# Graph network, edge convolutions: the gathers' waits moved from TensorE's counters to VectorE's

## The chip, the cores and the metric

The kernel runs on one core of a Trainium2 chip. The metric is device microseconds of one execution; the median of three runs is 2301.54 us (2296.12 to 2301.65). Four names are used for engines: TensorE (PE in the profile; PEld is its weight load), VectorE (DVE), ScalarE (ACT) and GpSimd (POOL). SP is the engine that only issues DMAs here.

## The reference, cut to what matters

There are 3125 nodes with 96 features and 53125 directed edges, sorted by destination. Four graph layers follow each other, each with a residual sum and a layer norm: two hops of normalised neighbour sums, two edge convolutions, sixteen hops with a teleport term, and two graph convolutions with a graph norm between them. The change is in the edge convolutions only:

```python
msg = x[src] @ W_msg + edge_attr @ W_edge             # one message per edge
agg = jax.ops.segment_max(msg, dst, num_segments=x.shape[0])
agg = jnp.where(jnp.isneginf(agg), 0.0, agg)
return agg + x @ W_root + b                           # leaky_relu behind it, twice in a row
```

## The kernel before, in words

A convolution is the function `edge_conv`, called twice. `x @ W_msg` is computed first for all nodes (`node_product`), kept in the on-chip memory (`y`, the tile `rows`) and also written to DRAM (`messages`), as two half-precision parts of 96 columns side by side. The edges are then walked in 26 turns (`N_IT`) of 16 tiles of 128 edges. The row `x[src] @ W_msg` of every edge of a tile is fetched in one of two ways:

- Eleven tiles of a turn (`FROM_POOL`) are gathered by GpSimd: one indirect DMA per tile (L1423) takes 128 rows from `messages` in DRAM into `conv_rows`. The tiles of a turn are j = 0 to 10; there are two sets of buffers, so the gathers of turn i + 2 go into the buffers of turn i.
- The five others (`TAKEN`) are taken by TensorE. VectorE writes one-hot matrices (L1540, 25 instructions a turn, in eight chunks: seven of three and one of four), TensorE multiplies them with `y` (L1473, 125 matmuls a turn, in the same eight chunks) and ScalarE evacuates the result (L1595). The one-hots lie in a ring of four slots (three of three tiles, one of four): VectorE may fill chunk h only when TensorE has finished chunk h - 4.

A message group is four tiles. TensorE starts it with the edge attributes (L1452) and adds the fetched rows with the identity (L1461, L1462). VectorE runs a segmented running maximum over it (L1550, the scan), TensorE turns the result back (L1500), and ScalarE evacuates it and stores it to DRAM (L1603, L1605). SP loads attributes and masks three groups ahead (L1374, L1376).

The order is written out by hand on each engine. For turn i, TensorE runs: message group 0, takes 0 and 1 of turn i + 1, message group 1, takes 2 and 3, the turn back of group 0, message group 2, takes 4 and 5, the turn back of group 1, message group 3, takes 6 and 7, the turn back of group 2. VectorE runs: scan 0, one-hots 4 and 5 of turn i + 1, scan 1, one-hots 6 and 7 of turn i + 1, scan 2, one-hots 0 and 1 of turn i + 2, scan 3, one-hots 2 and 3 of turn i + 2.

GpSimd runs only the gathers here, in order. From the third turn on (i >= 2), the first gather into each message group's buffers (j = 0, 4, 8) waits until the group two turns earlier has been computed. On top of that, every gather waits in `room(i - 2, j)`, which spreads the eleven gathers over a turn. It uses four counters. `s_msg` counts message groups, starting at 4. `s_scan` counts scans, starting at 4. `s_took` counts chunks of takes, seven a turn (the last chunk of a turn counts on another counter). `s_hot` counts chunks of one-hots, `NC` = 8 a turn. Before the change, with `step, late = divmod(j, 3)`, the gather waits for message group `step` of turn i - 2 if `late` is 0, and otherwise for chunk of takes 2 `step` + `late` - 1 of turn i - 1, which TensorE runs right behind that message group.

The gathers of the first two turns wait for none of this (turn 0) or for the first takes (turn 1). Behind the last gather, GpSimd fetches the first rows of the result, each waiting for late message groups and stores.

Of the kernel before, what the change touches and what calls it, by code (L numbers as in the profile page):

```python
# [60 lines left out]
GT = 4  # L61
# [6 lines left out]
NC = len(CHUNKS)  # L68
# [1247 lines left out]
def edge_conv(c, tag, y, result, head, sem, ends=False):  # L1316
# [14 lines left out]
    with ExitStack() as st:  # L1331
# [5 lines left out]
        def taken_rows(j, n):  # L1337
# [15 lines left out]
        s_zero, s_msg, s_scan, s_tr, s_back, s_hot, s_took, s_pair, s_evac = (  # L1353
            sem(f"{tag}_{n}") for n in ("zero", "msg", "scan", "tr", "back", "hot", "took", "pair", "evac"))
# [11 lines left out]
        with nc.Block(no_gpsimd_drain=True) as block:  # L1366
            @block.sync
            def _(sp):
                def load_group(i, g, width):
                    n = i * GT + g  # L1370
                    k = n % AHEAD
                    sp.wait_ge(s_msg, n + 1 + GT - AHEAD)
                    for q in (0, AE // 2):
                        sp.dma_start(attr[q:q + AE // 2, k, 0:width], halves_v[:, n * GW:n * GW + width]).then_inc(s_ea[k], 16)  # L1374
                    sp.wait_ge(s_scan, n + 1 + GT - AHEAD)
                    sp.dma_start(mk[:, k, 0:width], c["mask_d"][:, n * GW:n * GW + width].to_broadcast([F, width])).then_inc(s_mk[k], 16)  # L1376

                head.load_srcs(sp, 1, TE)
                if ends:
                    sp.wait_ge(s_none, 1)  # L1380
                    sp.dma_start(c["scan_d"][EP:EP + 1, :], none).then_inc(s_none, 16)
                for i in range(N_IT):
                    if i == 2:
                        if ends:
                            sp.wait_ge(s_ends, 1)
                        sp.dma_start(need[:, :], c["deg"][P - 1:P, :].bitcast(I32)).then_inc(s_need, 16)
                    for g in range(GT):
                        load_group(i, g, LEFT if i == last_it and g == GT - 1 else GW)
                        if g == 1 and i + 2 < N_IT:
                            head.load_srcs(sp, i + 2, LEFT_TAKEN if i + 2 == last_it else TE)  # L1390
                sp.wait_ge(s_pair, NB * N_IT)
                result.early(sp)

            @block.gpsimd
            def _(pool):
                for s in (s_msg, s_scan, s_tr, s_back):
                    pool.sem_inc(s, GT)
                for s in s_st:
                    pool.sem_inc(s, 16)
                pool.wait_ge(head.s_y, N_STORED)  # L1400

                def room(i, j):

                    step, late = divmod(j, 3)
                    if late == 0:
                        pool.wait_ge(s_msg, (i + 1) * GT + step + 1)
                    else:
                        pool.wait_ge(s_took, (i + 1) * (NC - 1) + 2 * step + late)

                def behind_first_takes(j):  # L1410

                    pool.wait_ge(s_took, 1 + j * (NC - 2) // (FROM_POOL - 1))

                for i in range(N_IT):
                    for g, tiles in enumerate(by_dma):
                        for j in tiles:
                            if i == 1:
                                behind_first_takes(j)
                            if i >= 2:
                                if j % GT == 0:  # L1420
                                    pool.wait_ge(s_msg, (i - 1) * GT + g + 1)
                                room(i - 2, j)
                            pool.indirect_dma_start(  # L1423
                                out=gat[:, i % 2, j, :], out_offset=None, in_=c["y_d"],
                                in_offset=bass.IndirectOffsetOnAxis(ap=idx_all[:, i * IT + j:i * IT + j + 1], axis=0),
                            ).then_inc(s_gat[i % 2][g], 16)

                pool.wait_ge(s_need, 16)
                if ends:
                    pool.wait_ge(s_none, 17)  # L1430
                pool.sem_inc(s_gate, 1)
                for k in range(2):
                    for g, tiles in enumerate(by_dma):
                        early = [k * FROM_POOL + j for j in tiles if k * FROM_POOL + j < EARLY]
                        if early:
                            stored = pool.value_load(need[0:1, early[-1]:early[-1] + 1], min_val=32, max_val=16 * (N_IT * GT // 2 + 1))
                            pool.wait_ge(s_msg, (N_IT - 2 + k) * GT + g + 1 + GT)
                            pool.sem_inc(s_gate, 1)
                            for parity in range(2):
                                pool.wait_ge(s_st[parity], stored)  # L1440
                                pool.sem_inc(s_gate, 1)
                            for t in early:
                                result.gather(pool, t)
# [481 lines left out]
```

## Time and profile before

| | |
|---|---|
| median of three runs | 2301.54 us |
| the profiled execution | 2304.43 us, span 2302.6 us |
| mean granted TensorE clock | 0.960 |
| TensorE, VectorE, ScalarE, GpSimd busy | 2030.8, 1240.7, 672.1, 759.0 us |
| the takes, L1473 | 639.2 us of matmuls, x6500 |
| the gathers of messages, L1423 | 578.3 us, x572 |
| the one-hots, L1540 | 346.3 us, x1300 |
| the scans, L1550 | 264.5 us, x208 |

The span runs from the first to the last instruction. The first convolution lies between about 286 and 760 us of it, the second between about 831 and 1306 us. Busy time of TensorE counts pipelined matmuls, so it says that the engine had work and not that it ran at its peak. "issue" as a releaser stands for idle time in which an engine waited for nothing that the profile shows, and "remote" for an event that the profile can't put to an instruction.

### The profile page before, as it was taken

The page shows a single profiled execution, that of the slowest core. Times are in us where ns is not written, and L with a number is a line of the kernel's source. Part 1 is how long each engine was busy: PE and PEld are TensorE (multiplying, and loading weights), DVE is VectorE, ACT ScalarE, POOL GpSimd, SP SyncE. Part 2 cuts the span into 40 slices and gives each one's busy share as a digit, 9 for nine tenths or more (in the row PEclk, how much of TensorE's full clock was granted, in tenths as well). Part 3 has the DMA queues.
Part 4 walks back from the last instruction along what each step waited for, and adds up shares of the span by engine and source line. Part 5 has one row for each costly group of instructions (what it writes and reads, how often), then busy time and mean ns, then how long its engine had stood idle before and what let it go on. Part 6 is the DMA issues. An engine that isn't in the chain of part 4 may idle for free. (4 is left out here: it accounts for less than half of the span.)

```text
span 2302.6 us, 57334 instructions
## 1 busy us (share of the span) xinstructions
PE 2030.8 (88%) x23524; PEld 1924.2 (84%) x23524; DVE 1240.7 (54%) x3485; ACT 672.1 (29%) x1939; POOL 759.0 (33%) x762
## 2 busy tenths in 40 slices
PE   4599688888888678888888699999999999999998
PEld 4499578777777567777777599999999999999988
DVE  8946366566565446666656474444444444444635
ACT  6824122222221212222222133332333333333434
POOL 2567366666555266656566510000000000000000
PEclk9999899999999789999999899999999999999999
DMA  3054445545554435555455400000000000000000
GB/s 75 1 164 131 106 123 137 132 132 132 131 133 117 122 87 134 134 131 133 130 132 130 126 17 2 2 2 2 2 2 2 2 2 2 1 2 2 2 2 23
DMA packets 153147, 163.58 MB, mean 71 GB/s; under 512 B 43697, under 2 KB 141612, under 8 KB 152885
## 3 DMA queue, kind: packets, MB, share of 16 engines
q1 hardware_dynamic: 100493, 83.89, 14.3%
q0 software_dynamic: 20464, 32.18, 7.5%
q10 hardware_dynamic: 31928, 43.84, 5.3%
q8 instruction: 186, 3.05, 0.5%
q14 instruction: 76, 0.62, 0.1%
HBM read 100.90 MB, written 58.89 MB: 69 GB/s over the span
## 5 line engine op out<-in xcount | busy, mean ns | idle before, releaser
L1473 PE MATMUL c_taken<-rows,conv_hot 125*128 125x192 f16 x6500 | 639.2, 253 | 102.7 <-issue 92.3
L1423 POOL DMA_INDIRECT conv_rows<-messages,idx_all x572 | 578.3, 1011 | 411.7 <-issue 121.6
L1473 PEld LDWEIGHTS c_taken<-rows,conv_hot 125*128 125x128 f16 x6500 | 555.7, 101 | 153.2 <-issue 137.3
L1540 DVE TENSOR_SCALAR conv_hot<-head_offset_srcs 125x640 f16<-125x640 f16 x1300 | 346.3, 328 | 272.2 <-DMA c_mask<-segment_mask 90.5
L1726 PE MATMUL l_ps<-rows,counts 125*128 125x192 f16 x5625 | 466.2, 246 | 1.9 <-DVE rows L1830 1.9
L1726 PEld LDWEIGHTS l_ps<-rows,counts 125*128 125x128 f16 x5625 | 464.0, 98 | 2.4 <-DVE rows L1830 2.4
L1726 PE MATMUL l_ps<-conv_rows,counts 125*128 125x192 f16 x5000 | 414.0, 246 | 0.8 <-DVE conv_rows L1871 0.8
L1726 PEld LDWEIGHTS l_ps<-conv_rows,counts 125*128 125x128 f16 x5000 | 412.6, 98 | 1.0 <-DVE conv_rows L1871 1.0
L1550 DVE TENSOR_TENSOR_SCAN c_scanned<-c_mask,c_scanned,c_msg 96x512 f32<-96x512 bf16 x208 | 264.5, 1272 | 151.0 <-DMA c_need<-deg 55.3
L1862 DVE SCALAR_TENSOR_TENSOR l_uf<-l_ps,l_cf,l_wide 125x96 f32<-125x96 f32 x400 | 127.1, 318 | 317.6 <-ACT l_wide L1797 317.6
L1603 ACT ACTIVATE c_back<-c_tr 128x384 f32<-128x384 f32 x208 | 102.0, 491 | 536.0 <-PE c_tr L1500 180.6
L1797 ACT ACTIVATE l_wide<-l_ps,l_cl 125x96 f32<-125x96 f32 x400 | 135.6, 339 | 294.3 <-PE l_ps L1726 286.5
L1500 PE MATMUL c_tr<-ident,c_scanned 96*128 96x96 f32 x832 | 112.1, 253 | 42.0 <-issue 34.9
L1462 PE MATMUL c_msg<-ident,conv_rows 128*96 128x128 f16 x728 | 118.0, 226 | 11.0 <-issue 10.7
L1461 PE MATMUL c_msg<-ident,conv_rows 128*96 128x128 f16 x728 | 117.4, 225 | 10.2 <-issue 10.0
L1500 PEld LDWEIGHTS c_tr<-ident,c_scanned 96*128 96x128 f32 x832 | 84.5, 144 | 49.0 <-issue 47.6
L1462 PEld LDWEIGHTS c_msg<-ident,conv_rows 128*96 128x96 f16 x728 | 88.3, 128 | 35.6 <-issue 17.6
L1868 DVE TENSOR_TENSOR l_uf<-l_uf,l_wide 125x96 f32<-125x96 f32 x400 | 103.0, 258 | 13.6
L1461 PEld LDWEIGHTS c_msg<-ident,conv_rows 128*96 128x96 f16 x728 | 90.6, 129 | 12.0 <-issue 11.9
L1595 ACT ACTIVATE conv_rows<-c_taken 128x384 f16<-128x384 f32 x104 | 42.8, 411 | 182.8 <-PE c_taken L1473 138.7
L1801 ACT ACTIVATE conv_rows<-l_uf 125x96 f16<-125x96 f32 x200 | 56.6, 283 | 135.5 <-DVE l_uf L1868 135.5
L1871 DVE SCALAR_TENSOR_TENSOR conv_rows<-conv_rows,l_uf 125x96 f16<-125x96 f16 x200 | 51.8, 259 | 69.9 <-ACT conv_rows L1801 69.9
(297 smaller groups left out, 1774.3 us busy)
## 6 DMA issues: line engine op xcount, KB each, us to landing
running_max<-c_back ACTq DMA_DIRECT2D x208, 192.0 KB
c_attr<-attr_halves SPq DMA_DIRECT2D x412, 64.0 KB
c_mask<-segment_mask SPq DMA_DIRECT2D x206, 96.0 KB
conv_rows<-messages,idx_all POOLq DMA_INDIRECT x572
head_srcs<-sources SPq DMA_DIRECT2D x50, 160.0 KB
l0a_raw<-in_ea_t SPq DMA_DIRECT2D x50, 132.8 KB, 2.3
attr_halves<-l0a_hi SPq DMA_DIRECT2D x50, 66.4 KB, 2.1
attr_halves<-l0a_lo SPq DMA_DIRECT2D x50, 66.4 KB, 2.1
```

What stands on the lines that cost most here:

```text
L1423: pool.indirect_dma_start(out=gat[:, i % 2, j, :], out_offset=None, in_=c["y_d"], in_offset=bass.IndirectOffsetOnAxis(ap=idx_all[:, i * IT ...
L1461: pe.matmul(to, row[:, 0:F], ident16[:, :], start=False, stop=False)
L1462: last = pe.matmul(to, row[:, F:2 * F], ident16[:, :], start=False, stop=(j == GT - 1))
L1473: return pe.matmul(acc[:, (NB * i + j // 2) % ACCS, j % 2 * (2 * F):(j % 2 + 1) * (2 * F)], hot[:, slot + k, j * ET:(j + 1) * ET], y[:, t, :],
L1500: last = pe.transpose(tr[0:ET, g % 2, j * F:(j + 1) * F], scanned[0:F, g % 2, j * ET:(j + 1) * ET], ident[0:F, 0:F])
L1540: last = v.tensor_scalar(hot[:, SLOTS[h % len(SLOTS)] + k, :], off[:, :], float(t * P - SRC_MID), None, ALU.is_equal)
L1550: v.tensor_tensor_scan(scanned[0:F, k, :], mk[:, n % AHEAD, :], msg[0:F, k, :], scanned[0:F, 1 - k, GW - 1:GW], ALU.add, ALU.max).then_inc ...
L1603: act.activation(back[:, g % 2, :], tr[0:ET, g % 2, 0:GT * F], ACT.Copy, scale=1.0 / YS).then_inc(s_back, 1)
L1726: return pe.matmul(ps[:, bank, at_col:at_col + 2 * F], at[:, k, t * P:t * P + 128], u[hop % 2][:, k, :], start=(k == 0 and at_col == 0), s ...
L1797: act.activation(clo[:, b, :], result(hop, t, 1), ACT.Copy, scale=(cl if hop < count else cl_next)[:, t:t + 1]).then_inc(s_clo, 1)
L1862: v.scalar_tensor_tensor(uf[:, t, :], result(hop, t, 0), (cf if hop < count else cf_next)[:, t:t + 1], clo[:, b, :], ALU.mult, ALU.add).th ...
L1868: v.tensor_tensor(uf[:, t, :], uf[:, t, :], xa[:, t, :], ALU.add).then_inc(s_uf, 1)
```

## The change

It replaces the two counters in `room`, which is called as `room(i - 2, j)` for every gather of turn i from the third turn on. If `late` is 0 the gather waits for scan `step` of turn i - 2, in place of message group `step`. Otherwise it waits for a chunk of one-hots: counted from chunk 0 of turn i - 1 it is chunk 3 + 2 `step` + `late`. For j = 1, 2, 4, 5 these are chunks 4, 5, 6, 7 of turn i - 1, and for j = 7, 8, 10 chunks 0, 1, 2 of turn i. The waits on `s_msg` for the buffers (j = 0, 4, 8) stay.

```diff
                     step, late = divmod(j, 3)
                     if late == 0:
-                        pool.wait_ge(s_msg, (i + 1) * GT + step + 1)
+                        pool.wait_ge(s_scan, (i + 1) * GT + step + 1)
                     else:
-                        pool.wait_ge(s_took, (i + 1) * (NC - 1) + 2 * step + late)
+                        pool.wait_ge(s_hot, (i + 1) * NC + 4 + 2 * step + late)
```

## Rows read from the trace of the kernel before

**Rows 1.** The page, part 1: busy us, share of span, instructions.
```profile
PE 2030.8 (88%) x23524; PEld 1924.2 (84%) x23524; DVE 1240.7 (54%) x3485; ACT 672.1 (29%) x1939; POOL 759.0 (33%) x762
```
**Rows 2.** Windows: stretch, length, busy us, PEclk, DMA share, GB/s.
```profile
323.80:727.90 404.10, 350.57 (x3897) 318.26 (x3896) 252.29 (x641) 86.95 (x177) 246.29 (x242) 0.96 0.52 132
870.00:1274.00 404.00, 348.18 (x3897) 314.48 (x3895) 251.46 (x638) 86.81 (x176) 243.56 (x242) 0.97 0.52 132
1310.00:2300.00 990.00, 969.83 (x11761) 963.92 (x11761) 447.68 (x1597) 324.20 (x1119) 13.05 (x12) 0.99 0.02 6
```
**Rows 3.** Groups by line, 323.8 to 727.9 us: busy, mean ns, idle before.
```profile
L1423 POOL DMA_INDIRECT conv_rows<-messages,idx_all x242 | 246.8, 1020 | 159.0 <-issue 53.3 <-remote 51.8 <-PE c_msg L1462 34.3
...
L1540 DVE TENSOR_SCALAR conv_hot<-head_offset_srcs 125x640 f16<-125x640 f16 x553 | 147.0, 327 | 100.4 <-remote 69.3 <-PE c_taken L1473 25.8 <-issue 3.3
L1550 DVE TENSOR_TENSOR_SCAN c_scanned<-c_mask,c_scanned,c_msg 96x512 f32<-96x512 bf16 x88 | 111.9, 1272 | 52.4 <-remote 40.5 <-PE c_msg L1462 9.2 <-issue 2.4
...
L1473 PE MATMUL c_taken<-rows,conv_hot 125*128 125x192 f16 x2750 | 266.5, 252 | 34.8 <-issue 29.3 <-ACT c_evacuated L1595 4.0 <-ACT conv_rows L1595 0.4
L1462 PE MATMUL c_msg<-ident,conv_rows 128*96 128x128 f16 x308 | 49.8, 226 | 4.2 <-issue 4.0
L1461 PE MATMUL c_msg<-ident,conv_rows 128*96 128x128 f16 x308 | 49.8, 225 | 2.8 <-issue 2.7
L1500 PE MATMUL c_tr<-ident,c_scanned 96*128 96x96 f32 x354 | 46.7, 249 | 10.0 <-issue 10.0
L1452 PE MATMUL c_msg<-c_attr,head_we 128*96 128x512 f16 x89 | 35.0, 393 | 1.8 <-issue 1.8
```
**Rows 4.** Lines L1540 and L1423: ns min/median/max, first and last start.
```profile
L1540 DVE TENSOR_SCALAR conv_hot<-head_offset_srcs x1300: 255/320/561, 253.9 to 1283.6; 125x640 f16<-125x640 f16 x186
...
L1423 POOL DMA_INDIRECT conv_rows<-messages,idx_all x572: 938/945/2523, 256.2 to 1274.6; - x191
```
**Rows 5.** Timeline of GpSimd: start us, us, instruction, idle before and releaser.
```profile
416.46 0.94 POOL L1423 DMA_INDIRECT conv_rows<-messages,idx_all  x1 [1.66 <-remote]
417.71 1.45 POOL L1423 DMA_INDIRECT conv_rows<-messages,idx_all  x1 [0.30 <-issue]
419.45 0.95 POOL L1423 DMA_INDIRECT conv_rows<-messages,idx_all  x1 [0.30 <-issue]
420.71 0.94 POOL L1423 DMA_INDIRECT conv_rows<-messages,idx_all  x1 [0.30 <-issue]
...
427.43 0.94 POOL L1423 DMA_INDIRECT conv_rows<-messages,idx_all  x1 [0.30 <-issue]
```
**Rows 6.** Timeline of VectorE, scans and one-hots of two stretches.
```profile
416.37 1.27 DVE L1550 TENSOR_TENSOR_SCAN c_scanned<-c_mask,c_scanned,c_msg 96x512 f32<-96x512 bf16 x1
417.56 1.48 DVE L1540 TENSOR_SCALAR conv_hot<-head_offset_srcs 125x640 f16<-125x640 f16 x6
420.37 1.27 DVE L1550 TENSOR_TENSOR_SCAN c_scanned<-c_mask,c_scanned,c_msg 96x512 f32<-96x512 bf16 x1 [1.34 <-remote]
...
439.70 1.27 DVE L1550 TENSOR_TENSOR_SCAN c_scanned<-c_mask,c_scanned,c_msg 96x512 f32<-96x512 bf16 x1 [2.41 <-remote]
440.90 1.71 DVE L1540 TENSOR_SCALAR conv_hot<-head_offset_srcs 125x640 f16<-125x640 f16 x7
...
446.31 1.77 DVE L1540 TENSOR_SCALAR conv_hot<-head_offset_srcs 125x640 f16<-125x640 f16 x6
```
**Rows 7.** Timeline of TensorE: a hole in the takes, a later message group.
```profile
428.39 0.49 PE L1473 MATMUL c_taken<-rows,conv_hot 125*128 125x192 f16 x4 [0.18 <-issue]
...
450.80 0.38 PE L1452 MATMUL c_msg<-c_attr,head_we 128*96 128x512 f16 x1
```
**Rows 8.** The page, DMA issues: KB each or us to landing.
```profile
counts<-edge_values,b_begin POOLq DMA_INDIRECT x5, 9.2
```
**Rows 9.** Timeline of all engines: a gather beside one-hots.
```profile
399.81 0.78 DVE L1540 TENSOR_SCALAR conv_hot<-head_offset_srcs 125x640 f16<-125x640 f16 x3
399.82 1.59 POOL L1423 DMA_INDIRECT conv_rows<-messages,idx_all  x1 [0.30 <-PE c_taken L1473]
```

## The prediction

> **What bounds the kernel now.** I read the page's busy times first [rows 1]: TensorE is busy for 88% of the span, VectorE for 54%, GpSimd for 33%. The change touches only the two convolutions, so the next view is the windows [rows 2]. They show 404.1 us and 404.0 us for the two stretches from the third to the twenty-fourth turn, each with 3897 matmuls. In each such stretch TensorE takes 2750 one-hot matmuls [rows 3], which is 22 turns of 125, so a turn lasts 404.1 / 22 = 18.37 us. Behind the convolutions, from 1310 us on, TensorE is busy 970 of 990 us, with 2% DMA [rows 2]; no gather of messages runs there, and nothing can change.
>
> The groups by line of the first stretch [rows 3] give each engine's load in one turn. GpSimd: 246.8 / 22 = 11.2 us of gathers. VectorE: (147.0 + 111.9) / 22 = 11.8 us, with (100.4 + 52.4) / 22 = 6.9 us idle. TensorE waits for no gather and for no one-hot: its idle time is put down to "issue" (29.3 + 4.0 + 2.7 + 10.0 + 1.8 = 47.8 us, or 2.2 us a turn) and to ScalarE's evacuation (4.4 us, 0.2 a turn). The timeline shows such an "issue" hole at 428.39 [rows 7]. So the conv is set by TensorE's own stream and by stalls that this trace cannot explain. GpSimd is a side queue, and the question is how much cover its gathers have.
>
> **What the change removes, adds and moves.** No instruction comes or goes: per conv, 24 turns x 11 = 264 gathers (528 of 572 in all) keep one wait each, against another counter. The four with j = 0, 3, 6, 9 wait for the scan behind the message group that they waited for; the seven others wait for the chunk of one-hots four chunks ahead of the chunk of takes that they waited for. By the code each new event lies behind the old one: the scan starts after its message group, and VectorE may fill a chunk's slots only after the very chunk of takes that the gather waited for (takes 0 and one-hots 4, takes 1 and one-hots 5, ..., takes 6 and one-hots 2 of the next turn). So every release comes later by the VectorE step, 1.27 us for a scan and 3 x 0.24 = 0.7 us or a little more for a chunk, and by whatever VectorE has queued ahead of it. It never comes earlier in itself.
>
> One turn, worked through. The gathers for the turn that starts at 447 start at 416.46, 417.71, 419.45 [rows 5]. The scan they would wait for ends at 416.37 + 1.27 = 417.64, the two chunks behind it at about 418.3 and 419.04 (417.56, six one-hots in 1.48), the next scan at 420.37 + 1.27 = 421.64 [rows 6]. A gather takes 0.94 us and the next starts 0.30 us behind its end [rows 4, 5]. The new starts are then 417.7, 418.95, 420.2 and 421.7: later by 1.2, 1.2, 0.75, and 1.0 against the fourth, which started when the queue was free. The middle ones gain less: those released by one-hots are already held by the queue ahead of them (427.43 would stay within 0.2 us [rows 5]). The last two and the next turn's first are again some 1.2 late. I take a mean of 0.6 us, with ends of 0 (all held by the queue) and 1.3 us (a full scan each).
>
> *What hides it.* The gather at 427.43 (j = 7) ends at 428.37 and feeds the second message group of its turn, which starts at 450.80 [rows 5, 7]: 22.4 us of cover. The message gathers' landing has no row; the longest median for another indirect gather is 9.2 us [rows 8]. 22.4 - 9.2 - 1.3 = 11.9 us are left. Cost on the path: 0. If the cover were gone, a shift would cost its own size once per turn at most, and only once per conv as a constant lag, for the lag doesn't add up as long as GpSimd keeps pace.
>
> *Does it keep pace?* It needs 11.2 + 11 x 0.30 = 14.5 us of 18.37 [rows 3, 5], so 3.9 us are free. Behind a waiting gather stand only gathers, and at the end those of the results, which wait for later message groups anyway. Nobody else waits for GpSimd there. Nothing is moved past SP's queue: its loads wait for the same counters as before.
>
> *What else moves.* The four scan-released gathers now start when VectorE turns to one-hots, and no longer beside the scan. Both kinds of meeting are in the trace already: a gather that started 0.01 us behind a one-hot took 1.59 instead of 0.94 us [rows 9], and one-hots run from 255 to 561 ns with a median of 320 [rows 4]. Bounds for one gather: 0 and +0.65 us on GpSimd; for its partner on VectorE: -0.06 and +0.24 us. The mean gather is 1.020 us long and the mean one-hot 0.327 [rows 3], so I take the small end on both: +0.1 us a gather, 1.1 us a turn out of GpSimd's 3.9, and under 0.1 us a turn for VectorE out of its 6.9 idle. Cost: 0. Gathers' packets move by half a microsecond in a conv whose DMA share is 0.52 [rows 2]; I bound that by plus or minus 0.1 us a turn and take 0.
>
> Here a rule bears on the change. The trace: a gather just behind the start of a one-hot was longer by 0.65 us, about a chunk of three [rows 9], but no one-hot was longer than 0.561 [rows 4]. The Trainium skill, "SBUF — State Buffer", section "Who interferes with whom", says that a VectorE operation in a two-port mode (tensor_scalar can be one) and a GpSimd operation shut each other out for the whole instruction, whichever came first. The first row agrees, the 0.561 does not: by the rule it should reach a gather's 0.94. By the rule's first half, all seven late gathers would be long ones: 11 x (0.945 + 0.30) + 7 x 0.65 = 18.3 us a turn, as good as the whole 18.37, so GpSimd would just keep pace and the cost would still be 0.
>
> **The sum.** 0 + 0 + 0 on the profiled execution's 2304.4 us (span 2302.6 and 1.8 around it). It stands 2.9 us above the median of 2301.5; the forecast is the median, 2302.
>
> **The rivals.**
> *S, slower: VectorE's one-hots stretch where VectorE sets the pace.* There are stretches in which VectorE has no wait: from 439.70 to 448.08 scans and one-hots follow each other directly [rows 6]. If each of the seven late gathers stretches one one-hot from 0.320 to 0.561, a turn gains 7 x 0.24 = 1.7 us of VectorE. The average turn swallows it; one in six may not: 8 x 1.7 = 14, so 2316. It decides from 0.14 us a turn over 48 turns. For it: the start of a gather is now tied to the start of the next one-hots. Against: TensorE shows no wait for one-hots at all [rows 3].
> *B, slower: the whole-instruction block.* If a gather that comes first shuts VectorE out for its 0.94 us, seven a turn add 6.6 us to 11.8: 18.4 us, the whole of today's turn, and any wait for TensorE comes on top. With 1 us of such waits, 48 x 1 = 48, so 2350. This is the second half of the rule above in the Trainium skill's "SBUF — State Buffer". Against it the 561 ns [rows 4].
> *F, faster: the "issue" stalls shrink.* If they have to do with when gathers fire, a twentieth to a fifth of 2.2 x 48 = 106 us might go; with a tenth, 2291. For it: they are the largest loss in the conv. Against: no row ties them to a gather, and two convs with different histories took 404.1 and 404.0 us.
> *N: the waits change nothing that can be seen.* Most gathers are held by the queue ahead of them and start where they did. Same time as my forecast, other reason: to be told apart by the starts.
>
> **How the numbers follow.** The forecast with N holds 0.64, F 0.15, S 0.17, B 0.04. A measurement of this kernel tells some 0.3% from no change, 6.9 us. Small drifts of the forecast beyond that are inside the shares: faster 0.17, same 0.62, slower 0.21. The range goes from F's 2290 to S's 2316 and leaves B and larger forms of F and S out, under 2 in 10.
>
> **What would show it right or wrong.** Right: gathers start about 0.6 us later against their scans, none before its scan's end; the idle time ahead of them is put down to VectorE; the message groups' idle stays without a gather; 22 turns in 404 us (401 to 407); the mean gather under 1.15 us, the mean one-hot at 0.32 to 0.34. Wrong: TensorE idle ahead of L1461 on a gather (the cover was not there), a mean one-hot above 0.36 with longer turns (S or B), or an "issue" idle in L1473 and L1500 that falls well under 40 us for the 22 turns (F).

## The result, and the profile after

The changed kernel takes 2368.38 us (median of four runs, 2362.52 to 2383.13) against 2301.6 us. The ratio is 1.0303, with an interval of 1.0278 to 1.0328: slower by 3.0%, and outside the range. The profiled execution took 2363.13 us, with a span of 2361.3 us; that is 58.7 us more than before. One of the ten runs of e17 below (2502.65 us, at a granted clock of 0.763) was slow and is left out of its ratio.

The first part of the page of the changed kernel answers to [rows 1]:

```profile
PE 2071.4 (88%) x23524; PEld 1956.1 (83%) x23524; DVE 1239.9 (53%) x3485; ACT 672.9 (28%) x1939; POOL 776.7 (33%) x762
```

VectorE and ScalarE work as long as before. TensorE is busy 40.6 us longer with the same number of matmuls, and the mean granted clock fell from 0.960 to 0.937.

```profile
core 0: 2361.3 us, clock 0.937
```

The windows of the third to the twenty-fourth turn of each convolution (columns as in [rows 2]):

```profile
324.00:756.70 432.70, 371.17 (x3896) 335.35 (x3895) 251.63 (x640) 87.04 (x177) 250.91 (x241) 0.90 0.49 123
902.10:1330.80 428.70, 364.19 (x3897) 328.25 (x3896) 251.17 (x639) 87.27 (x178) 255.21 (x242) 0.92 0.48 125
```

The same 22 turns take 432.7 and 428.7 us where they took 404.1 and 404.0 [rows 2]: 28.6 + 24.7 = 53.3 of the 58.7 us are here. A turn lasts 19.7 and 19.5 us instead of 18.37. The 53.3 us split in two: TensorE's busy time grew by 20.6 + 16.0 = 36.6 us for the same matmuls, and its idle time by the other 16.7 us. The clock is 0.90 and 0.92 instead of 0.96 and 0.97, so the first part is work at 1.2 in place of 2.4 GHz. The traces bear this out: at 2.4 GHz a matmul of these stretches adds 0.086 to 0.087 us of busy time in both kernels, and at 1.2 GHz 0.15 to 0.16; what grew is the number at 1.2, from 191 to 474 and from 136 to 368.

The groups by line of the first stretch (columns and order as in [rows 3]):

```profile
L1473 PE MATMUL c_taken<-rows,conv_hot 125*128 125x192 f16 x2750 | 282.7, 260 | 42.7 <-issue 41.5 <-ACT conv_rows L1595 0.5
L1423 POOL DMA_INDIRECT conv_rows<-messages,idx_all x241 | 252.4, 1047 | 182.1 <-issue 64.2 <-DVE c_scanned L1550 46.4 <-DVE conv_hot L1540 45.7
...
L1540 DVE TENSOR_SCALAR conv_hot<-head_offset_srcs 125x640 f16<-125x640 f16 x552 | 148.5, 329 | 135.0 <-remote 74.4 <-PE c_taken L1473 53.1 <-issue 7.0
L1550 DVE TENSOR_TENSOR_SCAN c_scanned<-c_mask,c_scanned,c_msg 96x512 f32<-96x512 bf16 x88 | 112.0, 1273 | 46.1 <-remote 36.1 <-PE c_msg L1462 6.0 <-issue 3.8
L1462 PE MATMUL c_msg<-ident,conv_rows 128*96 128x128 f16 x308 | 50.1, 227 | 4.7 <-issue 4.7
L1461 PE MATMUL c_msg<-ident,conv_rows 128*96 128x128 f16 x308 | 49.8, 227 | 1.9 <-issue 1.9
L1500 PE MATMUL c_tr<-ident,c_scanned 96*128 96x96 f32 x354 | 49.0, 258 | 7.7 <-issue 7.7
```

The mean gather is 1047 ns (1020 before) and the mean one-hot 329 (327). Of GpSimd's idle time 92 us are now put down to VectorE's two lines, as the diff says. No matmul waits for a gather. TensorE's idle time on "issue" grew, from 47.8 to 59.3 us (in its list of waits 41.5 for the takes, 7.7 for the turns back, 4.9, 3.3 and 1.9 for the message groups), and with it the mean take, from 252 to 260 ns.

What stands where such a hole lies? The timeline of GpSimd in the changed kernel shows seven gathers back to back, 0.30 us between two of them:

```profile
348.94 0.99 POOL L1423 DMA_INDIRECT conv_rows<-messages,idx_all  x1 [3.20 <-PE c_msg L1462]
350.23 1.34 POOL L1423 DMA_INDIRECT conv_rows<-messages,idx_all  x1 [0.30 <-issue]
351.88 0.96 POOL L1423 DMA_INDIRECT conv_rows<-messages,idx_all  x1 [0.31 <-issue]
...
356.90 0.95 POOL L1423 DMA_INDIRECT conv_rows<-messages,idx_all  x1 [0.30 <-issue]
```

TensorE's timeline beside it, from the last undisturbed takes on:

```profile
351.69 2.84 PE L1473 MATMUL c_taken<-rows,conv_hot 125*128 125x192 f16 x29
354.80 0.24 PE L1473 MATMUL c_taken<-rows,conv_hot 125*128 125x192 f16 x1 [0.27 <-issue]
...
356.29 0.29 PE L1500 MATMUL c_tr<-ident,c_scanned 96*128 96x96 f32 x1 [0.52 <-issue]
357.01 0.38 PE L1452 MATMUL c_msg<-c_attr,head_we 128*96 128x512 f16 x1 [0.43 <-issue]
...
359.15 0.34 PE L1461 MATMUL c_msg<-ident,c_evacuated 128*96 128x128 f16 x1 [0.36 <-issue]
...
359.60 3.73 PE L1473 MATMUL c_taken<-rows,conv_hot 125*128 125x192 f16 x22
```

And the windows before the holes, in them, and at the lower clock behind:

```profile
345.00:352.50 7.50, 6.46 (x81) 6.08 (x79) 5.12 (x14) 0.98 (x2) 3.69 (x4) 1.00 0.50 134
352.50:359.20 6.70, 4.15 (x33) 2.52 (x31) 1.75 (x3) 1.32 (x2) 4.13 (x5) 0.86 0.52 126
357.40:364.20 6.80, 5.92 (x37) 5.33 (x38) 3.66 (x10) 0.98 (x2) 3.37 (x5) 0.50 0.49 125
```

The train starts at 348.94 and its last gather ends at 357.85. From 354.5 to 359.15, so from 5.6 us behind its start to 1.3 us behind its end, TensorE gets one or a few instructions at a time, whatever they are: takes, turns back, message groups. 81 matmuls in 7.5 us become 33 in 6.7. Right behind it the granted clock is 0.50 (1.2 GHz) and 22 takes last 3.73 us, where 29 lasted 2.84.

I call gathers less than 0.35 us apart a train, and counted over both convolutions from the third turn on: 32 trains of five or more before, 54 after; pauses of over 0.25 us between the starts of two weight loads of TensorE (each less the 0.08 us of an undisturbed one), 195 us in all before and 219 after; time at 1.2 GHz, 136 us before and 249 after. The last four depend on where a convolution is taken to start and end, by up to 15 us; their differences, 24 and 113 us, hardly do. In the kernel before, a train of one gather had 0.12 us of such holes beside it on average, of three 0.80, of four 1.25, of five 2.07, of six 3.30. And at the start of its second convolution, where the wait under study doesn't apply yet, sixteen gathers run back to back from 803.0 to 822.7. The window of the kernel before:

```profile
805.00:838.00 33.00, 20.82 (x173) 16.23 (x172) 10.30 (x35) 1.92 (x4) 21.10 (x23) 0.72 0.27 60
```

173 matmuls in 33 us, at the rate of [rows 2] some 318, with all 12.2 us of idle time on "issue". So the trace of before held the mechanism; I had looked at one hole, and not at what GpSimd did ahead of it.

### The profile page after: what moved, and what is told of

Its sections match the earlier page's. It is cut to its first block and busy times, and to the rows that moved or that the text cites. A ratio compares the mean times of both kernels' runs of the same rounds, so it can differ in the third digit from the quotient of the medians.

```text
span 2361.3 us, 57334 instructions
## 1 busy us (share of the span) xinstructions
PE 2071.4 (88%) x23524; PEld 1956.1 (83%) x23524; DVE 1239.9 (53%) x3485; ACT 672.9 (28%) x1939; POOL 776.7 (33%) x762
## 5 line engine op out<-in xcount | busy, mean ns | idle before, releaser
L1473 PE MATMUL c_taken<-rows,conv_hot 125*128 125x192 f16 x6500 | 673.3, 260 | 132.6 <-issue 128.4
L1423 POOL DMA_INDIRECT conv_rows<-messages,idx_all x572 | 597.5, 1045 | 452.8 <-issue 155.4
L1473 PEld LDWEIGHTS c_taken<-rows,conv_hot 125*128 125x128 f16 x6500 | 578.3, 103 | 191.4 <-issue 178.5
L1540 DVE TENSOR_SCALAR conv_hot<-head_offset_srcs 125x640 f16<-125x640 f16 x1300 | 348.3, 329 | 339.7 <-PE c_taken L1473 132.9
L1461 PEld LDWEIGHTS c_msg<-ident,conv_rows 128*96 128x96 f16 x728 | 92.0, 131 | 14.3 <-issue 14.1
L1452 PE MATMUL c_msg<-c_attr,head_we 128*96 128x512 f16 x208 | 85.0, 409 | 7.3 <-issue 5.3
```

Source lines behind the costliest of these rows:

```text
L1423: pool.indirect_dma_start(out=gat[:, i % 2, j, :], out_offset=None, in_=c["y_d"], in_offset=bass.IndirectOffsetOnAxis(ap=idx_all[:, i * IT ...
L1461: pe.matmul(to, row[:, 0:F], ident16[:, :], start=False, stop=False)
L1473: return pe.matmul(acc[:, (NB * i + j // 2) % ACCS, j % 2 * (2 * F):(j % 2 + 1) * (2 * F)], hot[:, slot + k, j * ET:(j + 1) * ET], y[:, t, :],
L1540: last = v.tensor_scalar(hot[:, SLOTS[h % len(SLOTS)] + k, :], off[:, :], float(t * P - SRC_MID), None, ALU.is_equal)
```

## The experiments

The theory (T): gathers back to back starve TensorE's instruction stream, and the new releases make longer trains. Rivals: the gathers come too late (L); VectorE and GpSimd meet at the on-chip memory (P; the expectations below speak of its form with one-hots as V). Ratios are against the kernel before on the same chip.

**A train by itself, e1 (chip 12) and e5 (chip 4).** The gathers are added in the sixteen hops, where TensorE otherwise runs without a hole and there are no one-hots, scans or messages. `train(h, n)` puts n gathers into hop h; SP's twelve plain transfers are in hop 5:

```diff
...
+                train(2, 12)
+                train(3, 12, each_tile=True)
+                train(4, 12, kind="direct")
...
+                train(6, 12, kind="write")
+                train(7, 12, in_flight=1)
+                train(8, 12, in_flight=2)
+                train(9, 2)
+                train(10, 4)
+                train(11, 6)
```

> The kernel before, with gathers added to hops 2 to 11 of the sixteen-hop stage, where TensorE runs a matmul every 0.082 us with no hole and no other transfer is under way. The gathers fetch rows that nobody reads. Hop 2: 12 gathers back to back. Hop 3: 12 gathers, one per tile (2.06 us apart). Hop 4: 12 plain transfers of the same size from GpSimd. Hop 5: 12 plain ones from SP. Hop 6: 12 small memsets of GpSimd. Hop 7: 12 gathers, each waiting for the landing of the one ahead. Hop 8: at most two under way. Hops 9, 10, 11: 2, 4 and 6 back to back. Theory T (a long unbroken train of gathers starves TensorE): holes of 0.7 us in TensorE's stream in hop 2, some 6 to 9 us of them for 12 gathers, from 4 to 5 us behind the start to about 2.3 us behind the last start; about 0 for two, 1 for four, 3 for six; none or little in hops 3 and 7. Rival V (the gathers stretch one-hots and VectorE then holds TensorE): no one-hots here, so no hole in any hop. Rival L (lateness of the gathers): no hole, since nobody waits for them. Each hop lasts 51.7 us without holes.

The windows of e1, in this order: 12 gathers back to back; 12 gathers one per tile (2 us); 12 plain transfers from GpSimd; the same from SP; 12 gathers with at most two under way; then two, four and six gathers back to back.

```profile
1440.60:1457.80 17.20, 9.05 (x86) 6.92 (x84) 1.96 (x8) 1.53 (x5) 11.41 (x12) 0.80 0.17 35
1504.80:1529.00 24.20, 24.20 (x296) 24.20 (x294) 9.78 (x36) 7.21 (x24) 11.29 (x12) 1.00 0.13 27
1556.20:1567.00 10.80, 10.80 (x134) 10.80 (x132) 4.36 (x16) 3.12 (x10) 6.58 (x12) 1.00 0.23 57
1607.10:1615.00 7.90, 7.90 (x99) 7.90 (x97) 3.02 (x12) 2.50 (x8) 0.00 (x0) 1.00 0.36 77
1762.60:1783.00 20.40, 20.40 (x250) 20.40 (x248) 8.17 (x30) 6.24 (x20) 11.36 (x12) 1.00 0.14 31
1814.20:1819.00 4.80, 4.80 (x61) 4.80 (x59) 1.72 (x6) 1.45 (x5) 1.85 (x2) 1.00 0.09 21
1865.70:1872.00 6.30, 5.91 (x72) 5.69 (x71) 1.78 (x7) 1.59 (x5) 3.79 (x4) 1.00 0.17 35
1917.80:1927.00 9.20, 7.14 (x82) 6.40 (x80) 1.83 (x8) 1.59 (x5) 5.69 (x6) 1.00 0.15 34
```

Its timeline of TensorE over the first train, which ran from 1440.62 to 1455.37:

```profile
1437.80 8.33 PE L1776 MATMUL l_ps<-rows,counts 125*128 125x192 f16 x99
...
1447.83 0.33 PE L1776 MATMUL l_ps<-rows,counts 125*128 125x192 f16 x2 [0.97 <-issue]
1449.27 0.33 PE L1776 MATMUL l_ps<-rows,counts 125*128 125x192 f16 x2 [1.12 <-issue]
...
1457.77 2.56 PE L1776 MATMUL l_ps<-rows,counts 125*128 125x192 f16 x15 [0.92 <-issue]
```

Twelve gathers alone do it: 86 matmuls in 17.2 us, where an undisturbed row has some 210 (296 in 24.2). The same number one per tile costs nothing, and so do twelve that each wait for the landing of the one ahead (500 matmuls in 41 us). More bytes per second by plain transfers cost nothing (57 and 77 GB/s against 35), though GpSimd's twelve are the same 384 packets and 0.59 MB as the gathers. Twelve small memsets of GpSimd cost nothing either (76 matmuls in 6 us). So neither the one-hots nor the scans are needed, the bytes and packets moved are not enough, and P has nothing left to stand on: VectorE runs only what the hop gives it, and TensorE's idle time is all on "issue".

> The kernel before with added gathers in the sixteen-hop stage, nobody reads what they fetch. Hop 2: 12 gathers with one small memset of GpSimd behind each (a period of about 1.57 us in place of 1.25). Hop 3: 12 with two memsets each (about 1.9). Hop 4: 24 gathers of 64 rows back to back. Hop 5: 24 gathers of 128 rows with at most three under way. Hop 6: 8 back to back. Hop 7: 24 with one memset each. Hops 9, 10: 3 and 5 back to back. Theory T, a rate: TensorE starves only while gathers come faster than some period between 1.25 and 1.6 us, so no hole in hops 2, 3 and 7, holes of some 4 to 5 us for the eight and 1.5 for the five, none for the three, and in hop 5 as with a plain train of 24 (some 23 us), since three under way is what a plain train has. Rival Q, a count (any long run of gathers starves TensorE, if slowly): holes in hop 7, the 24 spaced ones, where hop 2 has none. For 64 rows: holes if it is the number of gathers, none or far fewer if it is rows per time and a 64-row gather is not half as long.

The windows of e5: 12 gathers with one memset between two (a gather each 1.35 us); 12 with two memsets (each 1.9 us); 24 of 64 rows; 24 with three under way; eight; 24 with one memset; three; five.

```profile
1443.70:1461.70 18.00, 11.16 (x99) 8.48 (x97) 2.26 (x9) 1.87 (x6) 12.94 (x24) 0.77 0.14 34
1508.50:1532.50 24.00, 24.00 (x293) 24.00 (x292) 9.70 (x36) 7.19 (x23) 14.27 (x36) 1.00 0.12 27
1560.10:1593.00 32.90, 11.33 (x87) 7.08 (x84) 1.71 (x7) 1.25 (x4) 21.59 (x24) 0.64 0.09 18
1639.70:1674.00 34.30, 12.83 (x97) 7.89 (x95) 2.64 (x10) 1.87 (x7) 22.66 (x24) 0.62 0.15 35
1720.10:1731.60 11.50, 8.02 (x81) 6.41 (x80) 1.77 (x7) 1.24 (x4) 7.56 (x8) 0.92 0.14 34
1779.20:1815.00 35.80, 22.30 (x163) 15.25 (x161) 4.49 (x16) 3.45 (x11) 25.82 (x48) 0.67 0.15 33
1906.80:1912.00 5.20, 5.20 (x66) 5.20 (x64) 1.98 (x7) 1.59 (x5) 2.84 (x3) 1.00 0.13 30
1958.20:1966.50 8.30, 7.04 (x84) 6.68 (x83) 2.30 (x8) 1.59 (x5) 4.69 (x5) 1.00 0.14 33
```

An undisturbed matmul takes 24.20 / 296 = 0.082 us. By the matmuls that are missing in each window, TensorE lost 0.4 us to a train of four (77 would fit in 6.3 us, 72 are there), 1.4 to five, 2.5 to six, 4.9 to eight, 10.1 to twelve and 25.8 to the 24 of 64 rows: about 1.25 us, a gather's own period, for each gather beyond the first three or four. Half the rows change nothing, so it is the number of gathers and not their bytes. At 1.35 us a gather it is there, at 1.9, and in e1 at a mean of 1.6 with two under way, it is not.

**Which half costs? e2 and e3 (chip 12, as e1).** Each has one of the two lines of the diff:

```diff
-                        pool.wait_ge(s_msg, (i + 1) * GT + step + 1)
+                        pool.wait_ge(s_scan, (i + 1) * GT + step + 1)     # e2: scans only
-                        pool.wait_ge(s_took, (i + 1) * (NC - 1) + 2 * step + late)
+                        pool.wait_ge(s_hot, (i + 1) * NC + 4 + 2 * step + late)     # e3: one-hots only
```

> Only the four gathers with j = 0, 3, 6, 9 wait for VectorE (the scan); the seven others wait for chunks of takes as before. Theory T: the trains are broken at seven of eleven gathers by TensorE's own progress, so little changes: 2300 to 2320, about a fourth of the 67 us. Rival V: the one-hots meet the scan-released gathers, those that used to run beside the scan: most of the 67 us, 2340 to 2368. Rival L (every release that comes later costs): 4/11 of it with the scans' larger delay, 2325 to 2340.

> Only the seven gathers that waited for takes wait for one-hots; the four others wait for message groups as before. Theory T: most of the slowing, 2335 to 2370, with longer trains (mean above 4 in place of about 3). Rival V: the scan-released gathers are where they were, less than half of it, 2300 to 2330. Rival L: 7/11 of it, 2335 to 2350, without longer trains.

2357.12 us for e2, ratio 1.0254 (1.0215 to 1.0293). 2328.73 us for e3, 1.0114 (1.0089 to 1.0140). The four scan releases cost more than the seven one-hot releases; I had it the other way round. The count of trains of five or more goes with it only in the rough: 60 in e2, 46 in e3, against 54 in the changed kernel, which costs more than either. Both times lie in the ranges of rival V, not in T's. Yet V doesn't fit the traces: the mean one-hot is 0.327 us in e2 and 0.329 in e3 (0.327 before), and nearly all of TensorE's idle time is on "issue".

**No release at all, e4 (chip 12).** The line `room(i - 2, j)` is taken out:

> The gathers of a turn wait only for their buffers (j = 0, 4, 8), nothing in between; each gather is earlier than before or the same. Theory T: trains of four and three or eleven at once, TensorE starved and its clock lower: slower than before, 2340 to 2420. Rival V: gathers and one-hots meet as often as before, 2300 to 2320. Rival L: gathers are earlier, so 2300 or faster.

2379.0 us, 1.0307 (1.0252 to 1.0362); holes of 233 us and 253 us at 1.2 GHz. The changed kernel is as slow as one in which only the buffers hold the gathers back. But this run doesn't have more long trains: 46 are threes and 65 fours, and only 18 have five or more. A turn's gathers mostly run as four, four and three with pauses of 1.0 to 1.4 us between, and one of over 3 us behind. By the prices of trains by themselves (e1, e5) its trains make some 110 us of holes and not 233, and those of the kernel before some 100 and not 195, an estimate. So pauses of that length don't end the effect here, and the cost doesn't follow the count of long trains. The number of pauses does better: the 572 gathers of both convolutions fall into 133 trains in e4, 135 in e2, 143 in the changed kernel, 156 in e3, 162 in e6 (next) and 181 in the kernel before, nearly the order of their times; only e6 is out of it. No run varies this number alone.

**Later, but by TensorE, e6 (chip 4).** Each gather waits for one more chunk of takes:

```diff
-                        pool.wait_ge(s_msg, (i + 1) * GT + step + 1)
+                        pool.wait_ge(s_took, (i + 1) * (NC - 1) + 2 * step + 1)
-                        pool.wait_ge(s_took, (i + 1) * (NC - 1) + 2 * step + late)
+                        pool.wait_ge(s_took, (i + 1) * (NC - 1) + 2 * step + late + 1)
```

> Every gather waits for a later event of TensorE: one chunk of takes further on than before, 1.3 us or more later. The wait is still for TensorE. Theory T (what matters is that releases stop when TensorE stops, so trains stay short): 2295 to 2310, the distribution of trains as before. Rival L (lateness in itself costs): slower by as much as the change under study, 2340 to 2370.

2291.22 us against 2303.79: 0.9948 (0.9932 to 0.9965). That is a little below T's range, and clear of the noise, though only 0.5%: this beats both kernels. Its gathers are the latest of all. At a gather's start TensorE has done on average 78 of its takes, counted from the start of the turn before the gather's own, in the kernel before, 88 in the changed one, 97 in e6, and 58 in e4, which has the earliest gathers and costs 3%. So L falls: lateness costs nothing. Its GpSimd timeline shows trains of three, of which there are 76:

```profile
401.11 0.99 POOL L1423 DMA_INDIRECT conv_rows<-messages,idx_all  x1 [1.21 <-remote]
402.40 0.94 POOL L1423 DMA_INDIRECT conv_rows<-messages,idx_all  x1 [0.30 <-issue]
403.65 0.94 POOL L1423 DMA_INDIRECT conv_rows<-messages,idx_all  x1 [0.30 <-issue]
405.85 0.99 POOL L1423 DMA_INDIRECT conv_rows<-messages,idx_all  x1 [1.26 <-remote]
```

**A rest behind each gather, e7 (changed kernel) and e8 (kernel before), chip 4.** One waited memset behind each gather, `rest(pool.memset(spacer[:, :], 0.0))`:

> The changed kernel with one memset of GpSimd (8 values per partition) behind each gather, so that the gathers come at least 1.57 us apart. Theory T: TensorE's holes mostly gone and the clock up, although GpSimd now needs 17.3 us a turn: 2240 to 2310, so the slowing of 67 us vanishes. Rival V (one-hots and gathers meet): the same number of meetings and a busier GpSimd, so 2360 or slower. Rival L: every gather later still, slower than 2368.

> The kernel before with the same memset behind each gather. Theory T: its own trains are broken too, holes fall from about 195 us in the two convolutions to under 80 and the clock rises; the turn is then bound by GpSimd's 17.3 us: 2235 to 2280, faster than both kernels. Rival V or L: not faster than 2300, and slower by up to 20 us since GpSimd has less room.

2370.16 us, 1.0282 (1.0244 to 1.0319), and 2324.43 us, 1.0097 (1.0068 to 1.0126). Neither is cured, against T's forecasts and in line with V's and L's. My 1.57 us a gather was wrong: the memset lies inside the gap of 0.30 us and the period becomes 1.35, at which e5 has holes too.

**At most two under way, e9 to e12 (chip 6).** Each gather waits until the one two before it has landed, in the changed kernel (e9), the one before (e10), e6's (e11) and one without `room` (e12):

```diff
+                            if i * FROM_POOL + j >= 2:
+                                landed(*divmod(i * FROM_POOL + j - 2, FROM_POOL))
```

> The changed kernel, with its waits for VectorE, and one more: each gather waits until the last but one has landed, so at most two are under way (about 1.6 us a gather in the added trains of the sixteen-hop stage, which left no hole). Theory T (only gathers without a pause hold TensorE up, whoever releases them): the slowing of 67 us vanishes, 2240 to 2310, and the holes of TensorE in the convolutions fall from about 219 us to under 100. Rival O (the order of release against VectorE's work is what costs, and the holes are a by-product): as the changed kernel, 2355 to 2380. Rival L: later still, slower.

> The kernel before with the same limit of two under way. Theory T: its holes of about 195 us go too, and the turn is bound by 11 x 1.6 = 17.8 us of GpSimd in place of 18.4: 2230 to 2285. Rival O: 2295 to 2310, since the order of release stays. If GpSimd is made the bound by more than the holes cost, 2300 to 2330, with TensorE waiting for gathers.

> The kernel that waits for TensorE one chunk later, with the limit of two under way. Theory T: as the kernel before with the limit, within 10 us of it. Rival O: as without the limit, 2285 to 2297.

> No pacing by any engine's progress (buffers only), but two under way at most. Theory T: the limit is enough, so the 79 us that the missing pacing cost go, 2235 to 2300. Rival O: slower than before, 2340 to 2380.

2423.75, 2426.49, 2423.87 and 2384.45 us against 2284.89: ratios of 1.0623 (1.0587 to 1.0660), 1.0634 (1.0599 to 1.0668), 1.0610 (1.0578 to 1.0643) and 1.0428 (1.0386 to 1.0469). TensorE's waits in e9, from 300 to 1300 us (total us, times, longest):

```profile
PE c_msg L1468 <- DMA conv_rows<-messages,idx_all: 203.8, 86, 5.5
```

The list has no "issue" wait of the takes any more, which are 113.4 us in the changed kernel's list over its convolutions. So the starving is gone, but GpSimd is now too slow for eleven gathers a turn, and the message groups wait for it. All four are slower than the kernel before, where T had forecast 2230 to 2310 us. The change costs nothing here, 2424 against 2426 us, but that doesn't show that the trains were its price: where the landing of gathers sets the pace, the engine that releases them matters little in any case, and e11 takes 2424 too.

**Two chips without holes, e13 to e18 (chips 5 and 13).** These chips came by the draw. The kernel before takes 2036.72 us (24 runs) and 2037.12 us (19 runs) on them. e13 is a third set of trains of 24; e14 and e18 (kernel before) and e15 (changed kernel) leave the eleventh gather of each turn from the third on out, e16 and e17 every gather from the third turn on (in all five a part of the result is then not computed):

```diff
+                            if i >= 2 and j == FROM_POOL - 1:     # e14, e15, e18
+                                continue
-                for i in range(N_IT):
+                for i in range(2):     # e16, e17
```

> The kernel before with added gathers, 24 to a train, in the sixteen-hop stage; nobody reads what they fetch. Hop 2: at most two under way. Hop 4: two memsets of GpSimd behind each, not waited for one by one. Hop 6: threes, each three waiting until the one ahead has landed. Hop 8: fours in the same way. Hop 10: three memsets behind each. Hop 12: twos. If a mean rate decides (theory R: TensorE is held up as soon as gathers average less than about 1.6 us), the trains under that mean have holes in proportion and the others none: none for the twos, threes and two under way, few for the fours. If only the length of an unbroken run decides (theory T as it stood), the fours have 8 holes of 0.6 us, one each, and the others none, whatever their mean.

> The kernel before, with the eleventh gather of each turn left out from the third turn on (its tile's messages use stale rows, so that part of the result is not computed). Theory R (the mean rate of gathers, about 1.6 us each, is what sets a turn's 18.4 us, through TensorE's holes): 1.6 us a turn less, 48 x 1.6 = 77, and 2215 to 2240. Rival B0 (TensorE's own stream bounds the turn and gathers cost it 0.3 us of holes each): some 15 us, 2280 to 2295.

> The changed kernel with the same gather left out. Theory R with trains: with a tenth less to fetch, both kinds of wait leave GpSimd pauses, so it gains more than the kernel before does: 2240 to 2290 where the changed kernel stands at 2368, and the price of VectorE's release falls from 67 us to 20 to 50. Rival B0: 2350, the price stays at 67.

> The kernel before without any gather of messages from the third turn on (the messages use stale rows, so the result is not computed). It shows what TensorE, VectorE and the other transfers need for a turn. Theory R and theory T: no holes with issue as the releaser, turns of 14.3 to 15.5 us, 48 x 3.2 = 150 us less, 2130 to 2165. Rival B0, or that the other transfers cause the holes: 2240 to 2290 with holes of over 1 us a turn.

> The run without gathers from the third turn on (stale rows, the result is not computed), again, since the chip that ran it first took 2037 us for the kernel before, with no hole in TensorE even beside trains of gathers. On a chip where the kernel before takes about 2300: theories R and T, 2030 to 2060, a turn of 14.9 us as on the other chip, so that the whole difference of 265 us between the chips is due to the gathers. If the other transfers hold TensorE up too, 2080 to 2250. On the other kind of chip: 2032 again.

> The run with ten gathers a turn (the eleventh tile's messages use stale rows), again for the same reason. On a chip where the kernel before takes about 2300: theory R (each gather costs TensorE about 1.6 us of wall time, so the mean rate sets the turn), 2215 to 2240. If TensorE's own 14.9 us a turn come on top of holes that begin only in long trains (theory T as it stood), the tenth gather less takes away about a third of a turn's 3.4 us of holes, 2240 to 2270. If neither, 2285 to 2300.

e13 on chip 5: TensorE is never idle over all six trains, and the clock is 1.00, even for 24 gathers at 1.37 us each and for bunches of four. Those two:

```profile
1283.30:1317.00 33.70, 33.70 (x411) 33.70 (x409) 13.39 (x49) 10.16 (x33) 26.47 (x72) 1.00 0.18 37
1489.50:1532.00 42.50, 42.50 (x518) 42.50 (x516) 17.14 (x62) 12.79 (x41) 22.75 (x24) 1.00 0.14 30
```

e14: 2033.03 us, 0.9977 (0.9960 to 0.9994); e15: 2031.82, 0.9976 (0.9964 to 0.9988); e16: 2032.48, 0.9989 (0.9973 to 1.0005); on chip 13 e17: 2031.33, 0.9977 (0.9966 to 0.9988); e18: 2030.7, 0.9978 (0.9962 to 0.9993). Here the gathers from the third turn on cost some 0.2%, all of them together, and before's and after's releases are equal within 1.2 us in the form with ten gathers. On what I had set out to learn (which of number and order of the gathers sets the turn), these six runs say nothing, since no train hurts there. That no train hurts is plain in e14 and e15 themselves: each runs up to 132 gathers back to back. GpSimd in e14, and the windows of e14 and e15 inside the first convolution:

```profile
402.71 0.95 POOL L1425 DMA_INDIRECT conv_rows<-messages,idx_all  x1 [0.30 <-issue]
403.97 0.94 POOL L1425 DMA_INDIRECT conv_rows<-messages,idx_all  x1 [0.30 <-issue]
...
340.00:600.00 260.00, 260.00 (x3220) 253.09 (x3218) 220.19 (x527) 72.37 (x145) 183.23 (x190) 1.00 0.66 168
340.00:600.00 260.00, 260.00 (x3220) 253.09 (x3218) 216.93 (x527) 72.88 (x147) 183.69 (x189) 1.00 0.65 168
```

TensorE is busy for the whole 260 us at the full clock. With 3897 / 22 = 177 matmuls a turn [rows 2], 3220 are 18.2 turns, so a turn lasts 14.3 us in place of 18.37. Both ways of release give the same. GpSimd's pace is the old one, 0.94 us and 0.30 between, so on these chips TensorE doesn't feel what starves it on the others.

## Why the prediction was wrong

**What was right.** The cover and the pace: no matmul waited for a gather, and later gathers did no harm (e6). Most gathers wait for VectorE as worked out (42.7 us of idle time stay on message groups, the waits for the buffers), and they come later, by some ten takes of TensorE on average. The meetings with one-hots: 0.329 us against 0.327, and the train of e1 needs no one-hot. The rule of the Trainium skill, "SBUF — State Buffer", section "Who interferes with whom", weighed for rivals S and B, was not what decided: the longest one-hot of the changed kernel is 0.578 us. Neither rival came true, and F, which tied the "issue" holes to the gathers, had the sign wrong. The 18.3 us a turn in the part on that rule should be 18.2; nothing hangs on it.

**The step that failed** is "Gathers' packets move by half a microsecond in a conv whose DMA share is 0.52; I bound that by plus or minus 0.1 us a turn and take 0", together with the sentence that the conv is set by "stalls that this trace cannot explain" and, under F, "no row ties them to a gather". I priced a gather by its packets and its own length. What it costs here is TensorE's issue, and that depends on how closely the gathers follow each other, not on what one of them moves. I had set no sign for an "issue" idle that grows: it went from 47.8 to 59.3 us. The turn went up by 1.3 and 1.1 us, not by 0 within 0.1. The same trace that I read could have shown it: the holes grow with the train, 0.12 us beside one gather and 3.30 beside six, and 173 matmuls in 33 us beside the sixteen at the start of the second convolution.

**Why the new releases hurt.** Shown: gathers close behind each other starve TensorE on the chips where the change costs 3% (e1, e5); the whole loss in the convolutions is TensorE's idle time on "issue" and its lower clock; the gathers of the changed kernel stand closer (143 trains against 181, 54 of five or more against 32); and on a chip where no train holds TensorE up, the change costs nothing, measured with ten gathers a turn (e15 against e14). Not shown: that the longer trains are the whole of it. e4 has few long trains and costs as much, the price of a train by itself doesn't add up to a convolution's holes, and e9 against e10 would come out even in any case. Argued only: why the gathers stand closer. TensorE's events are spread by its own work, a chunk of 15 takes being 1.4 us or so (29 in 2.84), and when a train starves TensorE its releases stop too, so the train ends. VectorE's releases come closer, a chunk of three one-hots in 0.7 us behind a scan [rows 6], which is faster than a gather's 1.25 us, and they come in bursts from chunks that TensorE had long freed; a queue of released gathers builds up and GpSimd runs it through.

**How it becomes 58.7 us.** The holes themselves are the smaller part (16.7 us of idle time in the two stretches). The larger (36.6 us) is the clock: behind a stretch like the one shown, 33 matmuls in 6.7 us, TensorE is granted 1.2 GHz, and it spent 113 us more at it.

**What stays open.** What the gathers hold up in TensorE's path: the profile says "issue" for it. The trace of e1 speaks against one candidate, instructions that come late from DRAM. Its DMA records have a queue of kind "instruction" with one packet of 16 KB for every 114 to 142 matmuls of the hops; it has one at 1443.06, 10.6 us behind the one ahead and before the first hole, and the next at 1464.99, with 120 matmuls between them. So those transfers stayed in step with the matmuls over the train. Why the four scan releases cost twice the seven others (e2, e3). Whether it is the number of pauses, their length or the rate over some microseconds that counts. What length of pause ends a train: alone, three gathers cost nothing, while in the kernel before the trains of three had 0.80 us of holes beside them, so what ran ahead of them seems to count, as in e4. Whether e6 gains from its threes or from fewer holes in another way: it has 30 trains of five and more, about as many as the kernel before, and 186 us of holes against 195. Why two of the chips show none of it. The changed kernel with its eleven gathers wasn't run on those.

## What to carry to other kernels

Where TensorE shows many short idle pieces on "issue", lay GpSimd's timeline beside it before pricing them at nothing: a lone train of three gathers did no harm here, and from the fourth or fifth on TensorE lost a gather's period for each. It may be better to release a side queue by the engine that its work disturbs, for then it brakes itself (argued, not shown); an event of another engine that says the same thing in the count can say it in bursts. Prices taken from a probe by itself need not add up in the kernel: those of e1 and e5 give less than half of the holes of e4. And when a stall bounds the stage, a change that only moves when other work fires isn't free because that work has slack.

## What the runs showed of the hardware

- Twelve 128-row gathers back to back left TensorE 86 matmuls in 17.2 us in place of some 210. Gathers of 64 rows do it as well (87 matmuls in 32.9 us, for 24 of them).
- Twelve plain transfers of GpSimd in 10.8 us and twelve of SP in 7.9 us did nothing of the kind (134 and 99 matmuls, no hole).
- Twelve gathers with at most two under way (1.6 us each), or with two memsets between (1.9 us each), left no hole; with one memset between (1.35 us each) they left 99 matmuls in 18.0 us.
- The same kernel took 2285 to 2304 us on three chips (4, 6, 12) and 2037 us on two others (5, 13). On chip 5, trains of up to 132 gathers leave no hole, in a turn of 14.3 us; on 5 and 13 the kernel takes 2032.48 and 2031.33 us without any gather from the third turn on. That the 265 us between the two kinds are what the gathers cost on the first one fits this, but was not measured there. A ratio measured on one kind needn't hold on the other.
